# Norms and weights for layer 1's attention made inside layer 0's mixture of experts; batch 3's residual moved into the first global round

## The chip, the cores and the metric

One core of a Trainium2 chip runs the whole program. The metric is the device time of one execution in microseconds; lower is better. TensorE (PE) multiplies matrices and turns tiles, DVE (VectorE) and ACT (ScalarE) do elementwise work and read PSUM, POOL (GpSimd) does elementwise work in SBUF, SyncE (SP) issues the loads and stores. Each engine works through its own queue in order, and semaphores join them.

## The reference, cut to what matters

Two transformer layers over `x` of shape 4 x 1024 x 128, float32. Each block has the form x = x + layernorm(block(layernorm(x))):

```
x = x + LN(L0_attention(LN(x)))           # 16 heads of 64, causal
x = x + LN(L0_mixture(LN(x)))             # 8 routed experts (top 2) + 2 shared, SwiGLU, hidden 256
x = x + LN(L1_attention(LN(x)))           # below
x = x + LN(L1_soft_mixture(LN(x)))        # 8 x 64 slots

L1_attention(h):                          # 16 heads of 8, 4 key/value heads
  h = h + global_latent_attn(rmsnorm(h, norm1_w))   # keys and values through a latent of 32, causal
  h = h + local_gqa_attn(rmsnorm(h, norm2_w))       # causal window of 32
rmsnorm(h, w) = h * rsqrt(mean(h*h) + 1e-6) * w
```

So before the first product of layer 1's attention for batch 0 there stand: the mixture's output of batch 0 with its layer norm and residual, a layer norm of x, and the root mean square norm. The factor `w` of the latter is multiplied into the rows of the projection weights.

## The kernel before, in words

`x` stays in SBUF as 32 blocks of 128 rows (`g.x`); batch b is blocks 8b to 8b+7. The program is four stages in turn, each with its own tiles and semaphores and each a block of five engine programs. A barrier of all engines stands between two blocks: no engine starts the next stage before every engine has ended this one.

`mixture_layer0` runs 80 units: 4 batches x 10 experts x 2 halves of 512 rows. In unit u TensorE makes the up products of u (`raise_`, into 5 banks `m_up`) and the down product of u-1 (`lower`, `m_down`), ACT the SiLU, DVE `m_glu` (L1110) and the weighing of u-1 (L1122, into `acc` for a batch's first expert and into `part` for the rest), POOL adds `part` to `acc` (L850). DVE's list puts pieces of layer norms between the units, by the unit's number i within the batch: the residual of batch b-1 at i = 4 to 10, and the norm that makes the next batch's `x_norm` at i = 11 to 16. A norm has these pieces: four statistics pieces of two blocks each (L56), the variance (six small operations, L62 to L69), a root on POOL (L90), two pieces of four normalised blocks (L74). Batch 3's residual has no later units to sit in; it follows the last weighing (`residual(BATCH - 1)` at the end of DVE's program), its root at the end of POOL's.

`layer1_attention` works in 8 rounds of 32 steps: rounds 0 to 3 are global attention of batches 0 to 3, rounds 4 to 7 local attention. Round r makes scores and output of its own batch and prepares round r+1; the order is written out by hand, step by step, on each engine. "Round -1" prepares batch 0 alone: DVE makes the layer norm of x into `hidden`, squares, sums and scales it into `normed` (POOL: L90, L1378), multiplies the norm weights into `w_in` (L1712), TensorE turns `normed` (L1428), ACT copies it (L1615), then come the latent product (L1443), four quarters of projection (L1459, L1460), the rotation (L1738, L1384), the heads' norms, the slots' high and low parts and their turns, and the first scores (L1514). POOL zeroes `values` and the slots (L1366 to L1374) in this round, between its roots. SyncE loads 16 small tensors at the stage's start; ACT begins with `wait_ge(zeroed, 9)` and `wait_ge(loaded, 256)`. In rounds 0 to 2 the first norm of batch r+1 stands at steps 0 to 4, its squares, sum and scaling at steps 5 and 6. POOL cuts the diagonal block of each step (L1397) in rounds 0 to 3.

Of the kernel before, what the change touches and what calls it, by code (L numbers as in the profile page):

```python
# [15 lines left out]
P = 128  # L16
# [727 lines left out]

M_ORDER = [*range(E_ROUTED, EXPERTS), *range(E_ROUTED)]
# [8 lines left out]
RESIDUAL_ROOT_AT, NEXT_ROOT_AT = 6, 13  # L754
part_user = lambda u: u - 2 if place_of_unit(u) > 1 else u - 4

# [11 lines left out]
def mixture_layer0(nc, g):  # L768
    with ExitStack() as ctx:
# [16 lines left out]
        acc = sb("acc", [P, NBLK, D])  # L786
        gates = sb("gates", [P, NBLK, EXPERTS])
        norm = NormTiles(ctx, nc, "m_norm")
        lg = sb("lg", [P, NB, E_ROUTED])
# [14 lines left out]

        small_loaded, b3_loaded = sem("small_loaded"), sem("b3_loaded")
# [13 lines left out]
        cols_of = lambda b, c: slice(b * SEQ + c * HALF, b * SEQ + (c + 1) * HALF)  # L819
        as_blocks = lambda t: t[:].rearrange("p (t n) -> p t n", t=4)  # L820
# [3 lines left out]
        with nc.Block() as block:  # L824
            @block.sync
            def _(sp):
# [16 lines left out]
                sp.dma_start(b3[E_ROUTED:EXPERTS, :], g.inputs["L0_ffn_sb3"]).then_inc(b3_loaded, 16)  # L843

            @block.gpsimd
            def _(pool):
# [11 lines left out]
                for s in range(M_UNITS + 1):  # L858
                    u, i = s - 1, s % M_WINDOW
                    if s and place_of_unit(u):  # L860
                        pool.wait_ge(weighed, u + 1)
                        add(u, acc[:, blocks_of(batch_of_unit(u), half_of_unit(u)), :], part[u % 2][:])
                    for b, c in b3_added_at(s):
                        pool.wait_ge(b3_kept, b * 2 + c + 1)
                        add((b, c), acc[:, blocks_of(b, c), :], b3_part[c][:])
# [5 lines left out]
                assert roots + 1 == 2 * BATCH, roots  # L871
# [148 lines left out]
            def _(dve):  # L1020
# [15 lines left out]

                def residual(b):
# [75 lines left out]
                def weigh(u):  # L1113
# [8 lines left out]
                    dve.tensor_tensor(part[u % 2][:] if p else acc[:, blocks_of(b, c), :], as_blocks(down[u % 2]),  # L1122
# [48 lines left out]
HEADS, KV, HD = 16, 4, 8  # L1171
GQ = HEADS // KV
LAT = 32
# [5 lines left out]
RMS_EPS = 1e-6  # L1179
# [85 lines left out]
def layer1_attention(nc, g):  # L1265


    with ExitStack() as ctx:
# [6 lines left out]
        g.hidden = ctx.enter_context(nc.sbuf_tensor("hidden", [P, NBLK, D], F32))  # L1275
        norm1 = NormTiles(ctx, nc, "norm1")
        both = lambda name, shape, dt=F32: [sb(f"{name}{i}", shape, dt) for i in range(2)]
        w_in, w_o, norm_w = both("w_in", [P, 192]), both("w_o", [P, D]), both("norm_w", [P, 1])
        cos, sin = both("cos", [P, NB, HD // 2]), both("sin", [P, NB, HD // 2])
        w_up = sb("w_up", [LAT, 2 * KV * HD])  # L1280
        rows_of = sb("rows_of", [P, 2])
        normed = sb("normed", [P, NB, D])
# [22 lines left out]
        loaded, scaled, zeroed, chain = sem("loaded"), sem("scaled"), sem("zeroed"), sem("chain")  # L1305
# [37 lines left out]
        LOADS = 16  # L1343

        with nc.Block() as block:
            @block.sync
            def _(sp):
                for layer, (wq, wk, wo, nw, rope) in enumerate((
                        ("g_wq", "g_kv_down", "g_wo", "norm1_w", "c_rope_g"), ("l_wq", "l_wk", "l_wo", "norm2_w", "c_rope_l"))):
                    sp.dma_start(w_in[layer][:, 0:D], g.inputs["L1_attn_" + wq]).then_inc(loaded, 16)  # L1350
                    sp.dma_start(w_in[layer][:, D:D + 32], g.inputs["L1_attn_" + wk]).then_inc(loaded, 16)
                    sp.dma_start(norm_w[layer][:], g.inputs["L1_attn_" + nw].rearrange("(p a) -> p a", a=1)).then_inc(loaded, 16)
                    if layer == 0:
                        sp.dma_start(rows_of[:], g.inputs["c_rows_of"]).then_inc(loaded, 16)
                        sp.dma_start(w_in[1][:, D + 32:D + 64], g.inputs["L1_attn_l_wv"]).then_inc(loaded, 16)
                        sp.dma_start(w_up[:, 0:32], g.inputs["L1_attn_g_k_up"]).then_inc(loaded, 16)
                        sp.dma_start(w_up[:, 32:64], g.inputs["L1_attn_g_v_up"]).then_inc(loaded, 16)
                    sp.dma_start(cos[layer][:], g.inputs[rope][0].rearrange("(t p) n -> p t n", p=P)).then_inc(loaded, 16)
                    sp.dma_start(sin[layer][:], g.inputs[rope][1].rearrange("(t p) n -> p t n", p=P)).then_inc(loaded, 16)
                    sp.dma_start(w_o[layer][:], g.inputs["L1_attn_" + wo]).then_inc(loaded, 16)  # L1360

            @block.gpsimd
            def _(pool):
# [12 lines left out]
                def input_root(x):  # L1376
                    pool.wait_ge(ss_ready, x + 1)
# [1063 lines left out]
```

## Time and profile before

| | us |
|---|---|
| median of 3 runs | 2453.27 |
| lowest, highest | 2449.4, 2456.77 |
| the profiled execution | 2459.24 |
| its span, first to last instruction | 2457.5 |
| TensorE busy in the span | 2214.6 |
| DVE, ACT, POOL busy | 1459.5, 1229.4, 1054.8 |
| mean granted clock of TensorE | 0.959 |

The mixture's units end at 1548 us and the first scores of layer 1's attention are at 1611 us of the span. The granted clock is a share of 2.4 GHz: 1.00 is the full level, 0.50 the lower one of 1.2 GHz. In the timelines, equal instructions in a row are merged into one line with their count.

### The profile page before, as it was taken

How to read it: one execution, taken by the hardware profiler on the slowest of the kernel's cores; microseconds unless marked ns; L12 is line 12 of the kernel's file. 1: busy time of each engine (PE TensorE's matmuls, PEld its weight loads, DVE VectorE, ACT ScalarE, POOL GpSimd, SP SyncE). 2: the span in 40 equal slices, each digit the busy share in tenths (PEclk: the TensorE clock that was granted, in tenths of full speed). 3: DMA queues.
4: the chain of work that ended last, by engine and by line, in shares of the span. 5: the costliest groups of instructions: out<-in, count | busy, mean ns of one | idle time of the engine just before them, and what ended most of it. 6: DMA issues, size and time to landing. Idle time of an engine off the chain costs nothing. (4 is left out here: it accounts for less than half of the span.)

```text
span 2457.5 us, 40332 instructions
## 1 busy us (share of the span) xinstructions
PE 2214.6 (90%) x15428; PEld 1400.2 (57%) x15428; DVE 1459.5 (59%) x3240; ACT 1229.4 (50%) x1796; POOL 1054.8 (43%) x980
## 2 busy tenths in 40 slices
PE   4999999999999999985999999489999988876787
PEld 2555565556555565545888888334444455555667
DVE  3677758775777757753666666535545555545533
ACT  2555545554465535541333333167777866644543
POOL 0677757775677757771323223323322311100001
PEclk9999999999999999997999999679999999998999
DMA  2000000000000000002000000000000000003001
GB/s 74 1 1 1 1 1 1 1 1 1 1 1 1 1 1 1 1 1 65 1 1 1 1 1 1 7 1 1 1 1 1 1 1 2 2 3 74 1 1 35
DMA packets 36322, 18.19 MB, mean 7 GB/s; under 512 B 16666, under 2 KB 33956, under 8 KB 36132
## 3 DMA queue, kind: packets, MB, share of 16 engines
q1 hardware_dynamic: 36132, 15.61, 2.5%
q8 instruction: 125, 2.05, 0.4%
q14 instruction: 65, 0.53, 0.1%
HBM read 13.50 MB, written 2.10 MB: 6 GB/s over the span
## 5 line engine op out<-in xcount | busy, mean ns | idle before, releaser
L311 POOL TENSOR_TENSOR a_first<-a_first,a_ring 128x512 f32<-128x512 f32 (+3 forms) x352 | 559.3, 1589 | 142.2 <-ACT a_ring L556 106.9
L1645 ACT ACTIVATE g_probsT<-g_s_ps 128x1024 f32<-128x1024 f32 (+2 forms) x448 | 368.9, 869 | 143.2 <-PE g_s_ps L1514 89.0
L556 ACT ACTIVATE a_ring<-a_st 128x768 f32<-128x768 f32 (+1 forms) x256 | 234.8, 917 | 263.0 <-PE a_st L463 263.0
L478 PE MATMUL a_o_ps<-a_ring,a_v 128*64 128x512 f32 (+3 forms) x1280 | 249.2, 485 | 3.2 <-POOL a_ring L293 2.2
L645 DVE RECIPROCAL a_row_inv<-a_row_inv 128x512 f32<-128x512 f32 x64 | 213.9, 3343 | 16.8 <-ACT a_row_inv L544 16.8
L993 ACT ACTIVATE m_silu<-m_up,m_b 128x512 f32<-128x512 f32 x160 | 110.1, 688 | 220.8 <-PE m_up L927 220.7
L623 DVE TENSOR_REDUCE a_part_max<-a_mx 128x2 f32<-128x1024 f32 x128 | 156.6, 1223 | 103.2 <-PE a_mx L434 100.1
L1545 PE MATMUL g_o_ps<-g_probsT,g_values 128*32 128x512 f32 (+5 forms) x2688 | 213.1, 430 | 5.2 <-POOL g_probsT L1397 5.1
L850 POOL TENSOR_TENSOR m_acc<-m_acc,m_part 128x512 f32<-128x512 f32 x72 | 99.2, 1378 | 271.1 <-DVE m_part L1122 271.1
L1397 POOL TENSOR_SCALAR_AFFINE_SELECT g_probsT<-g_probsT 128x512 f32<-128x512 f32 x128 | 89.0, 698 | 255.2 <-ACT g_probsT L1645 255.0
L1514 PE MATMUL g_s_ps<-g_qT,g_kT 64*128 64x512 f32 (+3 forms) x896 | 173.9, 436 | 27.1 <-ACT g_probsT L1645 21.3
L1110 DVE SCALAR_TENSOR_TENSOR m_glu<-m_up,m_b,m_silu 128x512 f32<-128x512 f32 x160 | 119.4, 749 | 111.1 <-ACT m_silu L993 106.2
L630 DVE CUSTOM_DVE_ANT_0 a_masked<-a_mx,mask_wide,a_part_max 128x256 bf16<-128x256 f32 (+3 forms) x256 | 128.4, 548 | 92.8 <-PE a_mx L434 92.4
L630 DVE CUSTOM_DVE_ANT_0 a_masked<-a_mx,mask_wide 128x256 bf16<-128x256 f32 (+3 forms) x256 | 112.8, 488 | 82.9 <-PE a_mx L434 82.9
L1514 PEld LDWEIGHTS g_s_ps<-g_qT,g_kT 64*128 64x128 f32 x896 | 77.9, 189 | 143.4 <-ACT g_probsT L1645 94.9
L941 PEld LDWEIGHTS m_down<-m_w,m_glu 128*128 128x128 f32 x1280 | 155.0, 191 | 6.3
L941 PE MATMUL m_down<-m_w,m_glu 128*128 128x128 f32 x1280 | 155.5, 275 | 0.0
L463 PE MATMUL a_st<-a_q_hi,a_k_hi 64*128 64x512 f32 (+3 forms) x768 | 151.2, 387 | 3.9 <-ACT a_shift L534 3.1
L434 PE MATMUL a_mx<-a_k_hi,a_q_hi 64*128 64x512 f32 (+3 forms) x768 | 142.1, 391 | 12.0 <-DVE a_largest L630 11.3
L463 PEld LDWEIGHTS a_st<-a_q_hi,a_k_hi 64*128 64x128 f32 x768 | 73.5, 185 | 113.8 <-ACT a_ring L556 79.1
L927 PE MATMUL m_up<-m_xT_hi,m_w_hi 128*128 128x512 f32 x320 | 135.8, 425 | 1.4 <-DVE m_xT_lo L1062 1.4
L463 PE MATMUL a_st<-a_q_lo,a_k_hi 64*128 64x512 f32 (+3 forms) x768 | 135.9, 345 | 0.0
(287 smaller groups left out, 4373.7 us busy)
## 6 DMA issues: line engine op xcount, KB each, us to landing
m_w<-in_L_ffn_rw SPq DMA_DIRECT2D x2, 1024.0 KB, 8.4
s_w<-in_L_ffn_w SPq DMA_DIRECT2D x1, 2048.0 KB, 10.6
s_w<-in_L_ffn_w SPq DMA_DIRECT2D x4, 512.0 KB, 10.5
out_x<-x SPq DMA_DIRECT2D x8, 256.0 KB, 2.3
m_w<-in_L_ffn_rw SPq DMA_DIRECT2D x2, 512.0 KB, 5.2
x<-in_L_attn_x SPq DMA_DIRECT2D x1, 512.0 KB, 4.3
a_outT<-in_L_attn_w_q SPq DMA_DIRECT2D x1, 512.0 KB, 5.2
a_outT<-in_L_attn_w_k SPq DMA_DIRECT2D x1, 512.0 KB, 6.1
```

Source lines behind the costliest of these rows:

```text
L311: pool.tensor_tensor(total[:, h, q:q + w], total[:, h, q:q + w], probs_of(n, u)[:, h, off:off + w], ALU.add).then_inc(added, 1)
L434: last = pe.matmul(mx_ps[:, h, off:off + w], q_hi[m % 2][rows_of(h), i * P:(i + 1) * P], k_hi[m % 2][rows_of(h), key:key + w], start=True, ...
L463: last = pe.matmul(out[:, h, off:off + w], a[rows_of(h)], r[rows_of(h)], start=i == 0, stop=i == len(todo) - 1)
L478: last = pe.matmul(o_ps[rows_of(h), first_q:first_q + w], v_half[n // 4 % 2][:, j, head:head + A_HD], probs_of(n, u)[:, h, off:off + w], s ...
L556: act.activation(probs_of(n, u)[:, :, 0:w], st_ps[u % 2][:, :, 0:w], ACT.Exp).then_inc(exp_done, 1)
L623: last = dve.tensor_reduce(part_max[:, i, :], mx_ps[:], AX.X, ALU.max)
L630: last = dve.tensor_tensor_reduce(masked[1 - part][:, h, 0:w], mx_ps[:, h, off:off + w], g.mask_wide[:, HALF - w:HALF], 1.0, so_far, ALU.a ...
L645: dve.reciprocal(row_inv[c][:], row_inv[c][:]).then_inc(inv_ready, 1)
L941: last = pe.matmul(down[u % 2][:, t * P:(t + 1) * P], glu[u % 2][h][:, t * P:(t + 1) * P], w3[:, e, h, :], start=h == 0 and t == 0, stop=h ...
L1514: last = pe.matmul(out, kT[r % 2][s // 2][rows, kb * P:(kb + 1) * P], qT[r % 2][rows, j:j + at_once, a:e], start=True, stop=True, skip_gro ...
L1545: last = pe.matmul(o_ps[place * SLOT:(place + 1) * SLOT, a:e], values[r % 2][:, kb, head_at(s, place) // GQ, :], probsT[(r * STEPS + n) % ...
L1645: act.activation(out, src.rearrange("p k (j n) -> p k j n", j=at_once), ACT.Exp, scale=float(HD) ** -0.5).then_inc(exp_done, 1)
```

## The change

`hidden`, `normed` and the attention's weights are now allocated and loaded before the mixture ends: a class `AttentionWeights` holds the loads, and the mixture's SyncE program issues them last. `hidden`'s blocks of batch 3 serve as the accumulator of the mixture's batch 3 (`sums_of`), so its unfinished residual can be carried into the attention. In batch 3's units DVE now makes batch 0's layer norm (i = 11 to 16), squares (17), sum (18), scaling (19), and both weight scalings (11, 12); POOL makes the two roots. In the attention, round -1 starts at the turn of `normed`; POOL zeroes `values` and slots at its step 0; ACT waits for `zeroed` 4 before step 12 and 9 before step 18, DVE for 9 at step 18. Round 0 gets batch 3's residual at steps 8 to 14, with its root on POOL at step 10. The other first norms (batches 1, 2, 3) stay where they were.

```diff
 # mixture_layer0
-        acc = sb("acc", [P, NBLK, D])
+        acc = sb("acc", [P, NBLK - NB, D])
+        sums_of = lambda b, c: (acc if b + 1 < BATCH else g.hidden)[:, blocks_of(b, c), :]
 # SyncE, after b3
+                g.weights.load(sp, g, attention_loaded)
 # POOL
                     if s < M_UNITS and (i == RESIDUAL_ROOT_AT and s >= M_WINDOW
-                                        or i == NEXT_ROOT_AT and s < M_UNITS - M_WINDOW):
+                                        or i == NEXT_ROOT_AT):
...
-                inverse_root(pool, norm, g.minus_half[:, 0:NB], roots)
+                    if s == M_UNITS - M_WINDOW + RMS_ROOT_AT:
+                        pool.wait_ge(rms_ready, 1)
+                        pool.tensor_tensor(rms_root[:], rms_sum[:], g.minus_half[:, 0:NB], ALU.pow).then_inc(root_ready, 1)
 # DVE
+                def norms_of_attention():
...
+                    def square():
+                        chain.settle()
+                        own.did(dve.tensor_tensor(g.normed[:], first, first, ALU.mult))
+                    def sum_up():
+                        own.settle()
+                        own.did(dve.tensor_reduce(rms_sum[:], g.normed[:], AX.X, ALU.add))
+                        own.settle()
+                        dve.tensor_scalar(rms_sum[:], rms_sum[:], 1.0 / D, RMS_EPS, ALU.mult, ALU.add).then_inc(rms_ready, 1)
+                    def scale():
+                        dve.wait_ge(root_ready, 1)
+                        own.did(dve.tensor_tensor(g.normed[:], first, rms_root[:].unsqueeze(2).to_broadcast([P, NB, D]),
+                                                  ALU.mult))
+                    return layernorm_parts(dve, chain, x_of, out_of, norm, norms[0] - 1)[:-1] + [square, sum_up, scale]
...
-                        nexts = norm_of(b + 1) if b + 1 < BATCH else []
+                        nexts = norm_of(b + 1) if b + 1 < BATCH else norms_of_attention()
...
+                    if b + 1 == BATCH:
+                        for k in {17: (7,), 18: (8,), 19: (9,)}.get(i, ()):
+                            nexts[k]()
+                        if i in (11, 12):
+                            scale_weights(i - 11)
                 weigh(M_UNITS - 1)
-                for piece in residual(BATCH - 1):
-                    piece()
 # layer1_attention: SyncE's program removed. POOL
-                        if x < BATCH and n == 2:
-                            inverse_root(pool, norm1, g.minus_half[:, 0:NB], x)
-                            if r < 0:
-                                zero_values()
-                        if x < ROUNDS and n == (1 if is_local(r) else 5):
+                        if x in NORM_COUNT and n == 2:
+                            inverse_root(pool, norm1, g.minus_half[:, 0:NB], NORM_COUNT[x])
+                        if r == 0 and n == 10:
+                            inverse_root(pool, norm1, g.minus_half[:, 0:NB], 1)
+                        if r < 0 and n == 0:
+                            zero_values()
+                            zero_slots()
+                        if 0 < x < ROUNDS and n == (1 if is_local(r) else 5):
                             input_root(x)
-                            if r < 0:
-                                zero_slots()
 # TensorE: turn_input waits for normed_ready only if x > 0; the waits on `scaled` are gone. ACT
-                act.wait_ge(zeroed, 9)
-                act.wait_ge(loaded, LOADS * 16)
...
+                        if r < 0 and n == 12:
+                            act.wait_ge(zeroed, 4)
+                        if r < 0 and n == 18:
+                            act.wait_ge(zeroed, 9)
 # DVE
+                    left_over = residual(BATCH - 1, 1) if r == 0 else []
...
+                        if left_over:
+                            for i in {8: (0, 1), 9: (2, 3), 10: (4,), 12: (5,), 13: (6,), 14: (7,)}.get(n, ()):
+                                left_over[i]()
```

## Rows read from the trace of the kernel before

**Rows 1.** page, part 1: busy us, share of the span, instructions of each engine
```profile
PE 2214.6 (90%) x15428; PEld 1400.2 (57%) x15428; DVE 1459.5 (59%) x3240; ACT 1229.4 (50%) x1796; POOL 1054.8 (43%) x980
```

**Rows 2.** waits of TensorE: who waited, for whom: us in total, times, longest
```profile
PE g_x_ps L1428 <- DVE g_normed L1732: 23.0, 1, 23.0
...
PE g_x_ps L1428 <- DVE g_k_slots L1777: 16.0, 1, 16.0
```

**Rows 3.** timeline of TensorE at the seam: start, duration, what, count, [idle before]
```profile
1571.40 1.97 PE L1428 MATMUL g_x_ps<-ident,g_normed 128*128 128x128 f32 x8 [22.96 <-DVE g_normed L1732]
1575.32 3.42 PE L1443 MATMUL g_x_ps<-g_normedT,g_w_in 128*32 128x512 f32 x4 [1.96 <-ACT g_normedT L1615]
1578.67 0.49 PE L1459 MATMUL g_x_ps<-g_w_in,g_normedT 128*128 128x128 f32 x2
...
1581.79 0.77 PE L1459 MATMUL g_x_ps<-g_w_in,g_normedT 128*128 128x128 f32 x2
```

**Rows 4.** timeline of DVE at the seam
```profile
1548.48 0.69 DVE L1122 TENSOR_TENSOR m_part<-m_down,m_gates 128x512 f32<-128x512 f32 x1 [1.09 <-PE m_down L941]
...
1557.97 1.64 DVE L56 BATCH_NORM_STATS2 norm_stats<-x 128x6 f32<-128x128 f32 x8 [0.54 <-PEq L824]
...
1570.12 1.22 DVE L1732 TENSOR_TENSOR g_normed<-hidden,g_rs_h 128x1024 f32<-128x1024 f32 x1 [1.54 <-POOL g_rs_h L1378]
...
1587.91 0.83 DVE L1738 TENSOR_TENSOR g_part<-g_qk,g_cos 128x640 f32<-128x640 f32 x1 [13.25 <-ACT g_values L1624]
```

**Rows 5.** timeline of POOL at the seam
```profile
1547.46 1.27 POOL L850 TENSOR_TENSOR m_acc<-m_acc,m_part 128x512 f32<-128x512 f32 x1 [3.25 <-DVE m_part L1122]
1549.25 1.26 POOL L850 TENSOR_TENSOR m_acc<-m_acc,m_part 128x512 f32<-128x512 f32 x1 [0.52 <-DVE m_part L1122]
...
1560.55 1.64 POOL L90 TENSOR_TENSOR norm_rstd<-norm_var,minus_half 128x8 f32<-128x8 f32 x1 [6.55 <-DVE norm_var L69]
...
1570.92 3.63 POOL L1374 MEMSET g_q_slots<- 128x1024 f32 x4
```

**Rows 6.** timeline of ACT at the seam
```profile
1574.58 1.08 ACT L1615 ACTIVATE g_normedT<-g_x_ps 128x512 f32<-128x512 f32 x2 [28.99 <-POOL g_q_slots L1374]
```

**Rows 7.** seam by stretch: length, busy PE, PEld, DVE, ACT, POOL, granted clock, DMA
```profile
1551.00:1554.50 3.50, 0.00 (x0) 0.00 (x0) 1.64 (x11) 0.00 (x0) 1.65 (x1) 0.52 0.00 0
1578.50:1581.80 3.30, 3.30 (x18) 2.37 (x17) 0.00 (x0) 1.14 (x3) 0.00 (x0) 1.00 0.00 0
1581.80:1587.20 5.40, 5.39 (x17) 3.95 (x16) 0.00 (x0) 1.10 (x4) 0.00 (x0) 0.51 0.00 0
```

**Rows 8.** timeline of DVE, batches 2 and 3 of the mixture
```profile
1429.67 2.10 DVE L74 TENSOR_SCALAR m_x_norm<-x,m_norm_mean,m_norm_rstd 128x128 f32<-128x128 f32 x4
...
1505.45 1.21 DVE L1045 TENSOR_TENSOR x<-x,m_acc 128x1024 f32<-128x1024 f32 x1
```

**Rows 9.** timeline of POOL, batch 3 of the mixture
```profile
1505.61 2.21 POOL L850 TENSOR_TENSOR m_acc<-m_acc,m_part 128x512 f32<-128x512 f32 x1 [2.08 <-DVE m_part L1122]
```

**Rows 10.** busy time in batch 3 of the mixture
```profile
1457.00:1548.00 91.00, 91.00 (x566) 80.69 (x565) 54.88 (x115) 31.35 (x45) 26.55 (x20) 0.99 0.00 1
```

**Rows 11.** timeline of TensorE, batch 2 of the mixture
```profile
1427.08 1.95 PE L941 MATMUL m_down<-m_w,m_glu 128*128 128x128 f32 x16
...
1431.63 1.95 PE L941 MATMUL m_down<-m_w,m_glu 128*128 128x128 f32 x16
```

**Rows 12.** timeline of SyncE's queue, last load of the mixture
```profile
1154.46 0.24 SPq L843 DMA_DIRECT2D m_b<-in_L_ffn_sb  x1
```

**Rows 13.** timeline of TensorE, global rounds 1 to 3
```profile
1784.09 1.09 PE L1428 MATMUL g_x_ps<-ident,g_k_slots 128*128 128x128 f32 x8
...
1827.05 1.09 PE L1428 MATMUL g_x_ps<-ident,g_normed 128*128 128x128 f32 x8
...
1879.65 1.09 PE L1428 MATMUL g_x_ps<-ident,g_k_slots 128*128 128x128 f32 x8
...
1921.45 1.09 PE L1428 MATMUL g_x_ps<-ident,g_normed 128*128 128x128 f32 x8
```

More of the change, by code:

```diff
@@ L742 @@
 TOP = 8
+HEADS, KV, HD = 16, 4, 8
+GQ = HEADS // KV
+LAT = 32
+RMS_EPS = 1e-6
 M_ORDER = [*range(E_ROUTED, EXPERTS), *range(E_ROUTED)]
@@ L803, in mixture_layer0 @@
         aux = ctx.enter_context(nc.psum_tensor("m_aux", [P, HALF], F32))
+        attention_loaded, rms_ready, root_ready = sem("attention_loaded"), sem("rms_ready"), sem("root_ready")
         small_loaded, b3_loaded = sem("small_loaded"), sem("b3_loaded")
@@ L1035, in norm_of, with scale_weights @@
                     return layernorm_parts(dve, chain, x_of, lambda blk: x_norm[:, blk, :], norm, norms[0] - 1)
+                def scale_weights(layer):
+                    w, scale = g.weights.w_in[layer], g.weights.norm_w[layer]
+                    if layer == 0:
+                        dve.wait_ge(attention_loaded, g.weights.LOADS * 16)
+                    width = 192 if layer else 160
+                    own.did(dve.tensor_scalar(w[:, 0:width], w[:, 0:width], scale[:], None, ALU.mult))
+                def norms_of_attention():
+                    norms[0] += 1
+                    x_of, out_of = lambda blk: g.x[:, blk, :], lambda blk: g.hidden[:, blk, :]
+                    first = g.hidden[:, 0:NB, :]
+                    def square():
[11 more added lines that the diff above has]
+                    return layernorm_parts(dve, chain, x_of, out_of, norm, norms[0] - 1)[:-1] + [square, sum_up, scale]
                 def residual(b):
@@ L1121, in weigh @@
                         dve.wait_ge(added, M_ADDED[part_user(u)])
-                    dve.tensor_tensor(part[u % 2][:] if p else acc[:, blocks_of(b, c), :], as_blocks(down[u % 2]),
+                    dve.tensor_tensor(part[u % 2][:] if p else sums_of(b, c), as_blocks(down[u % 2]),
                                       gates[:, blocks_of(b, c), expert_of_unit(u)].unsqueeze(2).to_broadcast([P, 4, D]),
@@ L1178 @@
 LOCAL_W = P + WINDOW
-RMS_EPS = 1e-6
 STEPS = KV * NB
@@ L1303, in layer1_attention @@
         x_ps = [ctx.enter_context(nc.psum_tensor(f"g_x_ps{i}", [P, HALF], F32)) for i in range(2)]
-        loaded, scaled, zeroed, chain = sem("loaded"), sem("scaled"), sem("zeroed"), sem("chain")
+        zeroed, chain = sem("zeroed"), sem("chain")
         ss_ready, rs_ready, normed_ready = sem("ss_ready"), sem("rs_ready"), sem("normed_ready")
@@ L1341, in x_read @@
                 eng.wait_ge(x_read_dve, READS_DVE[k])
-        LOADS = 16
+        NORM_COUNT = {1: 0, 2: 2, 3: 3}
         with nc.Block() as block:
[L1346 to L1360, printed above, removed]
             @block.gpsimd
@@ L1447, in project @@
                     x_read(pe, "input", x, 0, quarter // 2)
-                    if is_local(x):
-                        pe.wait_ge(scaled, 2)
-                    else:
+                    if not is_local(x):
                         x_read(pe, "latent", x, 0, quarter // 2)
@@ L1791, in add @@
                         norm_chain.did(dve.tensor_tensor(batch, batch, hidden_of(x), ALU.add))
-                    return layernorm_parts(dve, norm_chain, y_of, y_of, norm1, x)[:-1] + [add]
+                    return layernorm_parts(dve, norm_chain, y_of, y_of, norm1, count)[:-1] + [add]
                 for r in range(-1, ROUNDS + 1):
@@ L1797, in _ @@
                     local = is_local(r)
-                    norm_parts = first_norm(x) if x < BATCH else []
-                    ends = residual(r - 1) if r > BATCH else []
+                    norm_parts = first_norm(x) if x in NORM_COUNT else []
+                    left_over = residual(BATCH - 1, 1) if r == 0 else []
+                    ends = residual(r - 1, r - 1) if r > BATCH else []
                     for n in range(STEPS):
@@ L1813, in _ @@
                                 sum_input(x)
-                                if r < 0:
-                                    dve.wait_ge(loaded, LOADS * 16)
-                                    scale_weights(0)
                             if n == (2 if local else 6):
                                 scale_input(x)
-                                if r < 0:
-                                    scale_weights(1)
-                                    dve.wait_ge(zeroed, 9)
+                        if x < ROUNDS:
+                            if r < 0 and n == 18:
+                                dve.wait_ge(zeroed, 9)
                             if n == (13 if local else 15):
```

66 lines of the change are left out of this document (42 added, 24 removed).

## The prediction

> **What bounds the kernel now.** I read the page first. TensorE is busy for 90% of the span [rows 1], so time is won only where TensorE stands still, or where its own work runs at the lower clock. The second view is the list of what TensorE waited for, longest first: the longest single wait of the whole kernel, 23.0 us, is its first turn of `g_normed` in layer 1's attention, released by DVE, and a second one of 16.0 us follows for `g_k_slots` [rows 2]. Only then did I read the timelines, engine by engine, over the seam from 1548 to 1611 us, to see what fills the 23 us.
>
> The last `m_down` ends at 1571.40 - 22.96 = 1548.44 us [rows 3]. From there everything is one serial chain of small operations. DVE weighs the last unit, POOL adds it (ends 1550.51), DVE and POOL make batch 3's layer norm and DVE adds the residual (ends 1557.44), then comes the barrier (0.54 us to DVE's next operation), then the layer norm of batch 0, its squares, sum, root, and the scaling that ends at 1571.34; TensorE starts at 1571.40 [rows 3 to 5]. Between POOL's last add and `g_normed` ready are 1571.34 - 1550.51 = 20.83 us, of which 0.54 is the barrier.
>
> TensorE then turns `g_normed` (1.97 us), but ACT starts its copy only at 1574.58, after 29.0 us of idleness that POOL's memset of `g_q_slots` ends [rows 5, 6]. So a second wait lies behind the first: the zeroing of nine tiles, which POOL queues behind its two roots. The latent product starts at 1575.32, 3.92 us after TensorE began, the projections at 1578.67, and DVE's rotation at 1587.91 [rows 3, 4].
>
> The clock is the third thing. TensorE is granted the lower level (1.2 GHz, mean 0.52) from about 1551.1 on, after some 2.7 us without a matmul, the full level (2.4 GHz, 1.00) from 1578.5 to 1581.8, and the lower one again to 1587.2 although it was busy for 5.39 of those 5.40 us [rows 7].
>
> **The change, part by part.** The sum is made on the profiled execution, 2459.24 us for its span of 2457.5, 5.97 above the median of the runs (2453.27); I carry the difference over to the median.
>
> (a) Removed from the seam: the residual of batch 3, batch 0's layer norm, square, sum, root, scaling, and both weight scalings. After the change the block ends when POOL's last add ends. In place of 1571.40, TensorE can start at 1550.51 + 0.54 = 1551.05. I take no extra time for TensorE itself to get through the barrier: no row shows it starting straight behind one, SyncE and DVE do in about 0.5 us. Bounds 0 to 1.5 us, the upper end by the nearest dearer seam step, POOL's own 1.64 us root [rows 5].
>
> (b) The scaling of `g_normed` now sits in the last unit between the last two weighings. DVE would start it at 1547.3 (it follows the weighing before last) and needs 1.22 us, so it ends at 1548.52, where the last weighing began at 1548.48 [rows 4]: 0.04 late. But POOL's add of unit 78 (1547.46, 1.27 us) falls on it [rows 5]. The same pair exists in batch 3: DVE's residual add of 1.21 us at 1505.45, and beside it a POOL add that took 2.21 us and ended 1.16 us after DVE's [rows 8, 9]. So POOL's add of unit 78 ends at 1548.52 + 1.16 = 1549.68, its last add at about 1551.0, and TensorE starts at 1551.0 + 0.54 = 1551.55. Cost 0.5 us; bounds 0 and 1.5 (if POOL goes first and DVE stands behind it, the weighing is 1.2 to 1.5 late).
>
> (c) The rest in batch 3's units: eight statistics (1.64), six small operations, two halves of the normalisation (2.10 each, with POOL running beside them), square (1.2), sum (1.2), two weight scalings (0.6 to 0.8 each, by a quarter of the 2.10 for each 128 columns), two more POOL roots (1.64 each), in nine units [rows 4, 5, 8]. TensorE is busy for all 91.0 us of batch 3 from 1457 on, DVE for 54.9 [rows 10]: over 20 units of 4.55 us DVE has 1.8 us to spare in each. In batch 2's units the same norm stands at the same places. There two `m_down` groups start at 1427.08 and 1431.63, 4.55 us apart, although DVE starts such a half of 2.10 us at 1429.67 [rows 8, 11]. Square and sum are shorter than 2.10. Price 0: what hides it is that slack, and five banks of `m_up`, which let a late `m_glu` pass. If the cover were gone, it would be what exceeds the gap, 0.7 us for each of five units, 3.5 in all. POOL waits for `rms_ready` in unit 18 with only the next add behind it, 4.55 us later. Bounds 0 to 3.5.
>
> (d) The sixteen loads go to SyncE's queue in the mixture, behind `b3`, whose last issue is at 1154.46 [rows 12]; at about 0.47 us each they are issued by 1162.3, nearly 350 us before DVE's wait for them. Everything the experts need is ahead of them in the queue. Price 0; bounds 0 and 1. Their removal at the seam brings nothing by itself: they were not waited for last.
>
> (e) ACT no longer waits for `zeroed`, 9 and the loads before its first copy. With TensorE starting at T, ACT starts after the first four turns, T + 1.15 (half of 1.97 and 0.17 to get there), copies in 0.6, and the latent product starts at T + 1.85 in place of T + 3.92: 2.07 us won [rows 3, 6]. What is late next is TensorE's own work. The zeroing itself begins at T: two `values` memsets and the small ones take 2.1 us, and ACT wants them at the first projection, T + 5.4; the slots' five take 4.6 and end at T + 6.7, ACT wants them past T + 25. Hidden.
>
> (f) The clock over the first products. TensorE stood still for 3.1 us instead of 23.0, yet the level fell at 1551.1, before 1551.55 [rows 7], so turns and latent product are priced cold: 1.85 + 3.42 = 5.25 us from T to the projections (7.27 before) [rows 3]. Four quarters of projection follow. Two at full level took 1581.79 - 1578.67 = 3.12 us, two at the lower 5.4 [rows 3, 7]; 0.7 to the rotation. All cold: 10.8. All warm: 6.2. As before, half and half: 8.5. I take 8.5, since the same instructions come in nearly the same order, with bounds 6.2 and 10.8. Rotation: T + 5.25 + 8.5 + 0.7 = T + 14.45 = 1566.0, in place of 1587.91: 21.9 us earlier.
>
> (The Trainium skill, TensorE: Matmul & The Clock Gate, HAM oscillation, says that a long enough idle gap sends the array back to the cold clock and each group after it starts cold. By that, too, the turns are cold; its Part 1, What's actually happening, would have the clock stay warm once sustained work has brought it up, and the projections would then all be warm. The trace speaks against this: the level fell again at 1581.8 amid dense work [rows 7].)
>
> (g) From the rotation to the first scores the same operations run in the same order: 0, but the clock's changes may fall otherwise. The difference of two quarters, 2.3 us either way, is the bound.
>
> (h) Round 0 gains batch 3's residual in steps 8 to 14: eight statistics, six small operations, eight normalisations, one add of 1.23 us (some 6 us of DVE) and one root of 1.64 on POOL. POOL's root stands ahead of the cut of step 11, and waits for a variance that DVE reaches only after reading the first latent bank: TensorE's second product of that pair may come late by a microsecond. The nearest rows are the rounds themselves. From the turn of `g_k_slots` to the next round's turn of `g_normed` it takes 1827.05 - 1784.09 = 42.96 us with a first norm inside (the same DVE and POOL work but the add), and 1921.45 - 1879.65 = 41.80 without one [rows 13]. So such a norm costs 1.16; I take 1.0. Bounds 0 and 4 (one more cut late by 1.6 and a spell of lower clock behind it).
>
> Sum: 21.9 - 1.0 = 20.9 us. 2459.24 - 20.9 = 2438.3 for the profiled execution, 2453.27 - 20.9 = 2432.4 for the median.
>
> **Rivals.**
> 1. *The clock stays up through the projections.* For: the stretch idle is 3.1 us, not 23. Against: the fall at 1581.8. Worth 8.5 - 6.2 = 2.3 more, with a share of the first products up to 4: 2453.27 - 23.2 = 2430.1, at the best 2426.
> 2. *The clock stays down throughout.* For: latent product and turns are now packed otherwise against the clock's changes, and in the whole of 1603 to 1611 it was down. 2.3 less: 2434.7.
> 3. *Moved work shows in round 0 and in batch 3.* A wait takes the place of the one removed: POOL stands at the root of step 10 while TensorE needs the next cut, and the units with a scaling slip. (c) 2 of 3.5 and (h) 3 to 4 give 4 to 5 less: about 2437.
> 4. *The work is on the path wherever it stands.* This ends on the other side. It has one place, DVE's queue ahead of `m_glu` and of the bank reads. If nothing there were slack, 11.5 us in batch 3, 6 to 8 in round 0 and POOL's roots of 5 would all lengthen TensorE's time, 24 in all, more than the 21.9 won: 2455 to 2456. It decides from the point where more than nine tenths of the moved work is uncovered. The 4.55 us distance of units with a norm in them speaks against it.
> 5. *The chain at the seam is not shortened as said*, because TensorE gets through the barrier much later than DVE, or the input is ready late: 5 us lost, 2437 to 2438.
>
> **How the numbers follow.** Forecast (with the clock half and half, round 0 at 0 to 2) 0.50; rival 1 0.17; rival 2 0.14; rival 3 0.12; rival 5 0.05; rival 4 0.02. The predicted time is 2432.4. Medians of three scatter by some 2 to 3 us (the three runs lie between 2449.4 and 2456.77), so the range takes rivals 1 and 2 with that scatter and most of 3: 2426 to 2439. About 0.3%, 7.4 us, is what a measurement can tell from no change. Only rival 4 and some mishap of two others reach that bound: faster 0.97, within 0.015, slower 0.015.
>
> **What the changed profile would show.** TensorE's wait for DVE's `g_normed` gone, and about 3 us of idleness in its place, ended by the barrier (a: wrong if over 5). POOL's add of unit 78 near 2.2 us (b). `m_down` groups of batch 3 still 4.55 us apart, the last matmul as early against the first of the mixture as before (c). ACT's first copy about 1.15 us after TensorE's first turn, not ended by a memset (e). The granted clock over the four quarters decides among 6.2, 8.5 and 10.8 (f). The `g_k_slots` wait still near 16 us. Round 0, from its first scores to round 1's turn of `g_normed`, longer by about 1 us (h). A total saving below 15 us or above 27 would make the prediction wrong.

## The result, and where the time went

The changed kernel runs in 2436.64 us (median of 5, 2429.34 to 2438.66), the kernel before in 2455.56 (median of 5, 2449.4 to 2456.77): ratio 0.9918, 95% interval 0.9896 to 0.9941, or 14 to 26 us. The medians are 18.9 us apart; forecast were 20.9. (A ratio in this document is that to the kernel before, run in the same series; the two numbers behind it are its 95% interval.) The two profiled executions, 2459.24 and 2429.34 us, are 29.9 apart. That is more than the change did, and the first thing to do was to cut both into stages that begin and end with the same instruction of TensorE:

| stage (us) | before | after | after, 2nd trace | after, 3rd |
|---|---|---|---|---|
| start to first turn of the mixture | 1147.4 | 1143.5 | 1145.9 | 1147.4 |
| to the end of the last `m_down` | 401.05 | 401.39 | 401.21 | 401.40 |
| **to the first scores** | **62.52** | **40.48** | **40.52** | **40.50** |
| to round 1's turn of `g_k_slots` (round 0) | 77.56 | 74.83 | 77.95 | 74.80 |
| to round 2's | 95.57 | 96.00 | 92.93 | 92.79 |
| to round 3's | 95.56 | 95.59 | 92.33 | 92.52 |
| to round 7's | 262.76 | 260.66 | 262.43 | 262.37 |
| to the end of the span | 315.09 | 315.15 | 315.10 | 314.90 |

The third row is the change: 22.0 us, the same in all three traces of the changed kernel within 0.04 (of the kernel before there is one trace). The rest are differences of up to 4 us that come and go between executions of the same kernel; within one series of runs the executions of either kernel spread over 6 to 16 us. Two later series gave 23.8 us (2432.97 against 2456.77) and 22.3 us (2430.67 against 2452.95) between the medians.

Of the 22.0 us, 20.0 are TensorE's shorter wait before its first turn, 1.85 the way from there to the projections, and the rest, 0.2, lies behind them.

TensorE's timeline at the seam after the change (columns as in [rows 3]); the last `m_down` ends at 1544.89:

```profile
1541.16 3.73 PE L980 MATMUL m_down<-m_w,m_glu 128*128 128x128 f32 x32
1547.84 1.94 PE L1476 MATMUL g_x_ps<-ident,normed 128*128 128x128 f32 x8 [2.95 <-PEq L860]
1549.71 3.62 PE L1491 MATMUL g_x_ps<-g_normedT,g_w_in 128*32 128x512 f32 x4
1553.26 0.80 PE L1505 MATMUL g_x_ps<-g_w_in,g_normedT 128*128 128x128 f32 x2
...
1557.48 0.79 PE L1505 MATMUL g_x_ps<-g_w_in,g_normedT 128*128 128x128 f32 x2
...
1577.57 1.94 PE L1476 MATMUL g_x_ps<-ident,g_k_slots 128*128 128x128 f32 x8 [16.00 <-DVE g_k_slots L1820]
```

TensorE now stands still for 2.95 us in place of 22.96 [rows 3], and what ends it is the barrier, not `g_normed`. The latent product follows the turns at once, where 1.96 us had been waited for ACT's copy. The stage's second wait, the last line, kept its 16.0 us [rows 2].

DVE, POOL and ACT over the same stretch, three timelines (rows that answer to [rows 4], [rows 5], [rows 6]):

```profile
1543.76 1.22 DVE L1100 TENSOR_TENSOR normed<-hidden,m_rms_root 128x1024 f32<-128x1024 f32 x1
1544.93 0.69 DVE L1190 TENSOR_TENSOR m_part<-m_down,m_gates 128x512 f32<-128x512 f32 x1
1562.26 0.82 DVE L1781 TENSOR_TENSOR g_part<-g_qk,g_cos 128x640 f32<-128x640 f32 x1 [16.63 <-ACT g_values L1670]
```
```profile
1543.92 3.58 POOL L887 TENSOR_TENSOR hidden<-hidden,m_part 128x512 f32<-128x512 f32 x2 [1.49 <-DVE m_part L1190]
1547.80 1.84 POOL L1413 MEMSET g_values<- 128x1024 f32 x2 [0.31 <-POOLq L860]
```
```profile
1548.96 0.60 ACT L1661 ACTIVATE g_normedT<-g_x_ps 128x512 f32<-128x512 f32 x1 [6.92 <-PE g_x_ps L1476]
```

DVE scales `normed` right before the last weighing; POOL's two adds, merged in one row, take 3.58 us where they took 1.27 and 1.26: the first, beside the scaling, takes 2.18, the second 1.26. ACT's copy starts 1.12 us after TensorE's first turn does, while POOL still zeroes.

The granted clock over turns and latent product, the middle of the projections, and their last part (columns as in [rows 7]):

```profile
1547.80:1553.20 5.40, 5.36 (x12) 2.10 (x12) 0.00 (x0) 1.78 (x3) 5.34 (x8) 0.50 0.00 0
1553.90:1557.40 3.50, 3.50 (x19) 2.66 (x18) 0.00 (x0) 1.16 (x5) 0.44 (x1) 0.98 0.00 0
1557.50:1561.50 4.00, 4.00 (x13) 2.97 (x12) 0.00 (x0) 0.55 (x2) 0.00 (x0) 0.50 0.00 0
```

The pattern is that of before: the lower level up to the projections, full in their middle, lower again although TensorE is busy for 4.00 of 4.00 us.

The moved work in batch 3's units, with TensorE's `m_down` groups around it (two timelines, as [rows 8] and [rows 11]):

```profile
1525.57 2.11 DVE L74 TENSOR_SCALAR hidden<-x,m_norm_mean,m_norm_rstd 128x128 f32<-128x128 f32 x4
...
1534.66 1.22 DVE L1090 TENSOR_TENSOR normed<-hidden 128x1024 f32<-128x1024 f32 x1
```
```profile
1522.98 1.95 PE L980 MATMUL m_down<-m_w,m_glu 128*128 128x128 f32 x16
...
1527.53 1.95 PE L980 MATMUL m_down<-m_w,m_glu 128*128 128x128 f32 x16
...
1532.07 1.95 PE L980 MATMUL m_down<-m_w,m_glu 128*128 128x128 f32 x16
...
1536.62 1.95 PE L980 MATMUL m_down<-m_w,m_glu 128*128 128x128 f32 x16
```

The groups stay 4.55 us apart, through a half of the normalisation of 2.11 us (between the first two) and the squares of 1.22 (between the last two).

### The profile page after: what moved, and what is told of

Its sections match the earlier page's. It is cut to its first block and busy times, and to the rows that moved or that the text cites. A ratio compares the mean times of both kernels' runs of the same rounds, so it can differ in the third digit from the quotient of the medians.

```text
span 2427.6 us, 40333 instructions
## 1 busy us (share of the span) xinstructions
PE 2205.2 (91%) x15428; PEld 1396.5 (58%) x15428; DVE 1457.3 (60%) x3240; ACT 1228.7 (51%) x1796; POOL 1056.3 (44%) x980
## 5 line engine op out<-in xcount | busy, mean ns | idle before, releaser
L887 POOL TENSOR_TENSOR m_acc<-m_acc,m_part 128x512 f32<-128x512 f32 x54 | 74.8, 1386 | 205.0 <-DVE m_part L1190 205.0
L463 PE MATMUL a_st<-a_q_hi,a_k_lo 64*128 64x512 f32 (+3 forms) x768 | 135.2, 344 | 0.0
```

The costliest lines, as they stand in the source:

```text
L463: last = pe.matmul(out[:, h, off:off + w], a[rows_of(h)], r[rows_of(h)], start=i == 0, stop=i == len(todo) - 1)
```

## Experiments

All are edits of the changed kernel; "stretch" is that from the last `m_down` to the first scores.

**1. The changed kernel again**, twice, to learn what repeats.

> The changed kernel once more, unaltered. Mine: the stretch from the last m_down to the first scores of the attention (62.5 us before the change, 40.5 after) is fixed by its chain and comes out at 40.5 within 0.3; the other stages, the 2.7 us less of round 0 among them, are the clock's changes falling otherwise and come out anew within 3 us. Rival: the 2.7 us less of round 0 (74.8 from first scores to the next turn of g_k_slots, against 77.6) belongs to the change and shows again within 0.3. Total 19 to 22 us below the kernel before by both.

> The changed kernel unaltered, as the partner of the two others in this call. Mine: TensorE idle for 2.95 us, the clock falls within them and the stretch is 40.5, as in its earlier traces; 4 to 5 us slower than the other two. Rival: the clock stays up here at times too, and then the stretch is 36.3.

Measured: stretch 40.52 and, in the later series, 40.50; round 0 77.95 and 74.80 (table above). The 22.0 us repeat. The first total lies 23.8 us below the kernel before, a little more than the 19 to 22 expected. The 2.7 us less in round 0 came in two of three traces, so they are not the change's. The second expectation held for the stretch, 40.50 with idleness of 2.95 us and the cold pattern, but not for the total: 2430.67 us lies 2.1 below that of experiment 6's version in the same series and 2.3 above the combination of experiment 7, not 4 to 5 above both.

**2. Batch 3's residual back at the seam.**

```diff
+                inverse_root(pool, norm, g.minus_half[:, 0:NB], roots)
...
                 weigh(M_UNITS - 1)
+                for piece in residual(BATCH - 1):
+                    piece()
...
-                        if r == 0 and n == 10:
-                            inverse_root(pool, norm1, g.minus_half[:, 0:NB], 1)
...
-                    left_over = residual(BATCH - 1, 1) if r == 0 else []
+                    left_over = []
```

> The changed kernel with batch 3's residual back behind the last weighing, at the seam. Mine: its layer norm, root and add stand in the chain with their full 6.9 us, so the stretch from the last m_down to the first scores is 47.4 (40.5 + 6.9), TensorE's idleness 9.8 in place of 2.95, and round 0 gives nothing back, since the residual lay hidden there: total 6.9 above the changed kernel. Rival from my prediction: round 0 gets 1 us shorter, total 5.9. Rival 2, that the chain was partly covered by the barrier and the start of TensorE: 4 to 5 in the stretch.

The added root stands at the end of POOL's program. Measured: 2440.93 us (ratio to before 0.994, 0.9916 to 0.9963), stretch 47.46, 6.94 more than the changed kernel's 40.52 in the same series (forecast 6.9); the medians are 8.0 apart. Round 0 took 77.87 us, against 77.95 with the residual in it. TensorE's first turn in its timeline waits 10.06 us, 7.1 more than 2.95:

```profile
1555.25 1.94 PE L1478 MATMUL g_x_ps<-ident,normed 128*128 128x128 f32 x8 [10.06 <-PEq L860]
```

The whole of this chain was on the path at the seam, and neither rival held.

**3. Batch 0's norms back in round -1.** The pieces `norms_of_attention` and POOL's two roots go from the mixture; `first_norm(0)`, `square_input(0)`, `sum_input(0)`, `scale_input(0)` and their roots come back.

> The changed kernel with batch 0's layer norm, squares, sum, root and scaling back in the attention's round -1 (the weight scalings stay in the mixture, the zeroing stands behind the two roots on POOL, ACT still waits late for it). Mine: 13.4 us of chain come back, less the 0.5 that the scaling costs in the last unit: 53.4 from the last m_down to the first scores; the mixture's batch 3 gets no shorter than by 0.4. Rival: the moved work cost TensorE time among the units too (up to 3.5), then batch 3 is shorter by that and the total rises by only 10.

Measured: 2440.30 us (0.9943, 0.9922 to 0.9964), 7.3 above the changed kernel of the same series; stretch 50.75, not 53.4. TensorE's idleness is what was forecast, 15.85 us, 12.90 more than 2.95. What gave 2.7 us back is the clock: 0.9 between first turn and projections, 1.8 in the projections. TensorE's first turn, and the granted clock over latent product and projections of this kernel:

```profile
1564.50 1.97 PE L1472 MATMUL g_x_ps<-ident,normed 128*128 128x128 f32 x8 [15.85 <-DVE normed L1770]
```
```profile
1566.40:1569.00 2.60, 2.60 (x5) 0.47 (x4) 0.00 (x0) 1.18 (x2) 1.25 (x2) 0.68 0.00 0
1569.00:1575.50 6.50, 6.50 (x33) 4.92 (x32) 0.00 (x0) 2.24 (x7) 0.00 (x0) 0.95 0.00 0
```

The full level came early in the latent product and stayed through the projections (mean 0.95), all four in 6.5 us. Without batch 0's norm in them, batch 3's units and the rest of the mixture took 401.52 us, with it 401.39, 401.21 and 401.40: the moved work cost TensorE nothing there.

**4. ACT waits for all nine memsets first.**

```diff
                 HIGHS = {18: 0, 19: 1, 20: 2, 21: 3, 22: 4}
+                act.wait_ge(zeroed, 9)
```

> The changed kernel, but ACT waits for all nine memsets before its first copy, as it did before the change. Mine: the memsets end 6.6 us after TensorE's start, ACT's first copy starts then in place of at 1.1, so the stretch from the last m_down to the first scores is 5.5 longer: 46.0. That is more than the 2.07 us that this wait cost in the kernel before, as the norms no longer hide it. Rival: it costs about 2 us, as it did, since the cold clock stretches what TensorE does in between anyway.

Measured: 2438.49 us (0.9925, 0.9902 to 0.9949), stretch 48.35, 7.8 more, not 5.5. ACT's copy starts 6.53 us after the first turn:

```profile
1547.88 1.94 PE L1476 MATMUL g_x_ps<-ident,normed 128*128 128x128 f32 x8 [2.95 <-PEq L860]
1555.15 3.59 PE L1491 MATMUL g_x_ps<-g_normedT,g_w_in 128*32 128x512 f32 x4 [5.34 <-ACT g_normedT L1661]
```
```profile
1554.41 1.08 ACT L1661 ACTIVATE g_normedT<-g_x_ps 128x512 f32<-128x512 f32 x2 [12.33 <-POOL g_q_slots L1421]
```
```profile
1555.10:1569.50 14.40, 14.31 (x36) 8.52 (x36) 0.00 (x0) 3.22 (x10) 0.00 (x0) 0.50 0.00 0
```

The wait cost 5.4, as forecast (POOL's memsets end 6.5 us after TensorE's start), and 2.4 more went to the clock, which stayed at the lower level for latent product and projections alike. So the rival's 2 us did not hold: the early copy was worth 5 us or more once the norms no longer hid the zeroing, though its row before showed only 2 us.

**5. The residual left out** (statistics to add; batch 3's output is then not the reference's).

```diff
-                    left_over = residual(BATCH - 1, 1) if r == 0 else []
+                    left_over = []
...
-                        if r == 0 and n == 10:
-                            inverse_root(pool, norm1, g.minus_half[:, 0:NB], 1)
```

> The changed kernel without batch 3's mixture residual (its statistics, variance, root, normalisation and add in round 0 are left out, so batch 3 is computed wrongly). Mine: round 0 (from first scores to the next turn of g_k_slots) stays at one of its two lengths, 74.8 or 77.6 to 78.0, as the clock falls, and TensorE's waits in it are the same; the total stays within 1 us of the changed kernel. Rival, the term of my prediction: round 0 is 1 us shorter than at the same clock, 73.8.

Measured: 2433.0 us (0.9921, 0.9889 to 0.9952). The changed kernel was not run in this series, so that the total stays within 1 us of it is not shown. Round 0 took 76.17 us, neither of the two lengths expected, so length alone doesn't settle it. Length beside the granted clock does. Round 0 as one stretch, in the order with residual (the changed kernel, then `zero_first`) and without (this one, then `residual_back`):

```profile
1585.37:1660.20 74.83, 66.62 (x493) 28.18 (x493) 43.08 (x109) 56.10 (x64) 27.11 (x31) 0.95 0.00 1
```
```profile
1593.27:1670.81 77.54, 70.18 (x492) 28.95 (x493) 43.07 (x109) 56.07 (x64) 27.19 (x31) 0.90 0.00 1
```
```profile
1591.11:1667.28 76.17, 67.97 (x493) 28.60 (x493) 37.12 (x86) 56.15 (x64) 25.60 (x30) 0.93 0.00 1
```
```profile
1592.65:1670.52 77.87, 69.88 (x493) 28.82 (x493) 37.37 (x86) 56.12 (x64) 25.63 (x30) 0.91 0.00 1
```

With it DVE is busy for 43.1 us, without for 37.1 to 37.4; the round's length goes with the clock instead. TensorE's idleness, the length less its busy time, is 8.21 us in the first line (with) and 8.20 in the third (without). At equal clock: the kernel before, without, 77.56 at 0.90, and `zero_first`, with, 77.54 at 0.90; `residual_back`, without, 77.87 at 0.91, and the second trace of the changed kernel, with, 77.95 at 0.91. TensorE's two longest waits in round 0 (us in total, times, longest) are the same with it (first) and without:

```profile
PE g_s_ps L1560 <- ACT g_probsT L1691: 6.3, 9, 1.6
PE g_o_ps L1591 <- POOL g_probsT L1444: 1.5, 1, 1.5
```
```profile
PE g_s_ps L1558 <- ACT g_probsT L1689: 6.3, 9, 1.6
PE g_o_ps L1589 <- POOL g_probsT L1444: 1.5, 1, 1.5
```

**6. Everything one unit earlier in batch 3**, so that no scaling stands in the last unit; run in two series.

```diff
-RESIDUAL_ROOT_AT, NEXT_ROOT_AT, RMS_ROOT_AT = 6, 13, 18
+RESIDUAL_ROOT_AT, NEXT_ROOT_AT, RMS_ROOT_AT = 6, 13, 17
...
-                        for k in {11: (0, 1), 12: (2, 3), 13: (4,), 15: (5,), 16: (6,)}.get(i, ()):
+                        late = {15: (5,), 16: (6,)} if b + 1 < BATCH else {14: (5,), 15: (6,)}
+                        for k in ({11: (0, 1), 12: (2, 3), 13: (4,)} | late).get(i, ()):
...
-                        for k in {17: (7,), 18: (8,), 19: (9,)}.get(i, ()):
+                        for k in {16: (7,), 17: (8,), 18: (9,)}.get(i, ()):
```

> The changed kernel with the two halves of batch 0's normalisation, the squares, the sum and the scaling each one unit earlier in batch 3 (14 to 18 in place of 15 to 19). Mine: no DVE work stands between the last two weighings, POOL's add of unit 78 is back at 1.3 us in place of 2.2, and TensorE's idleness at the seam goes from 2.95 to 2.4; stretch from the last m_down to first scores 40.0. Rival: POOL's last add is late for another reason (the second of the two adds itself), and it stays 2.95.

> The kernel of unit_earlier once more (batch 0's scaling out of the last unit; TensorE idle for 2.42 us at the seam). There the granted clock did not fall, and the stretch from the last m_down to first scores was 35.7 in place of 40.5. Mine: this belongs to the shorter idleness and comes again: 35.7, with the clock at the full level through turns, latent product and projections; total 4 to 5 us below the changed kernel of the same call. Rival: it was chance how the idleness of 2.4 us fell against the clock's changes; in some runs the clock falls as with 2.95 us, and the stretch is 40.0, the total 0.5 to 2.5 below.

Measured: first series 2428.46 us (0.9913, 0.9882 to 0.9944), stretch 35.73; second series 2432.74 (0.9915, 0.9889 to 0.9941), stretch 37.24. POOL's two adds and TensorE in the first trace, then TensorE in the second, the first trace's granted clock up to the projections' end (columns as in [rows 7]), and last the second trace's granted clock just before and behind the start of its first turn:

```profile
1544.56 1.27 POOL L887 TENSOR_TENSOR hidden<-hidden,m_part 128x512 f32<-128x512 f32 x1 [2.33 <-DVE m_part L1190]
1546.34 1.26 POOL L887 TENSOR_TENSOR hidden<-hidden,m_part 128x512 f32<-128x512 f32 x1 [0.51 <-DVE m_part L1190]
```
```profile
1547.95 1.06 PE L1477 MATMUL g_x_ps<-ident,normed 128*128 128x128 f32 x8 [2.42 <-PEq L860]
1549.36 1.88 PE L1492 MATMUL g_x_ps<-g_normedT,g_w_in 128*32 128x512 f32 x4 [0.34 <-ACT g_normedT L1662]
```
```profile
1551.41 1.94 PE L1477 MATMUL g_x_ps<-ident,normed 128*128 128x128 f32 x8 [2.42 <-PEq L860]
1553.28 2.65 PE L1492 MATMUL g_x_ps<-g_normedT,g_w_in 128*32 128x512 f32 x4
```
```profile
1547.90:1551.20 3.30, 2.90 (x13) 1.25 (x13) 0.00 (x0) 1.67 (x3) 3.23 (x6) 1.00 0.00 0
1551.30:1557.50 6.20, 6.16 (x32) 4.58 (x32) 0.00 (x0) 2.21 (x7) 3.15 (x4) 1.00 0.00 0
```
```profile
1551.30:1551.41 0.11, 0.00 (x0) 0.03 (x1) 0.00 (x0) 0.00 (x0) 0.04 (x1) 1.00 0.00 0
1551.41:1551.50 0.09, 0.09 (x1) 0.09 (x2) 0.00 (x0) 0.00 (x0) 0.09 (x1) 0.51 0.00 0
```

The adds are back at 1.27 and 1.26, as expected, and the idleness at 2.42 us in both. The stretch missed the expected 40.0: the 4.8 us less of the first trace are 0.53 of idleness and 4.2 of clock, which did not fall at all before the projections ended. In the second trace it stayed at the full level through the 2.42 us and fell just as the turns began, and they took 1.94 in place of 1.06. So my expectation for the repeat fell. Its rival was right that the clock may fall here too, but not in the numbers: the stretch is 37.24, not 40.0, as the full level was back for the projections, and the total lies 2.1 above the changed kernel of its series, not below it.

In the traces with 2.95 us of idleness or more, read in windows of 0.1 us, the clock fell 2.1 to 2.7 us after the end of the last `m_down` (changed kernel: 2.34, 2.15 and 2.36; kernel before: 2.69). TensorE resumed at 2.42 here, in the midst of these, and at 2.95 in the changed kernel, behind them all. What decides it at 2.42 us, these two traces don't show.

**7. Extra matmuls that keep TensorE busy.** Eleven behind the last `m_down`; then eight, together with edit 6.

```diff
                 lower(M_UNITS - 1)
+                for _ in range(11):
+                    pe.matmul(up[0][:], w_hi[:, 0, 0, 0:P], xT_hi[:, 0:HALF], start=True, stop=True)
```

> The changed kernel with eleven more matmuls of 128x512 (2.5 us in all, into a bank nobody reads) on TensorE behind the last m_down, while POOL's adds end. Mine: what the 3 us of idleness cost is the clock. With it bridged the turns and the latent product run at the full level: 3.3 us from the first turn to the projections in place of 5.4, and the projections at 6.2 to 8.4; stretch from the last m_down to first scores 37 to 38.5. Rival: the clock falls on the turns themselves, a weak load, so the granted clock is at the lower level by the latent product again, and less than 1 us is won.

> unit_earlier with eight extra matmuls of 128x512 (1.9 us) behind the last m_down as well. Mine: TensorE is idle for some 0.5 us, the clock stays up in every run, stretch 35.7 as in unit_earlier; total equal to unit_earlier within 0.5 if the clock stays up there by itself, up to 4 us faster in the median if there it does so only at times. Rival: the extra matmuls overrun POOL's end and cost their excess, up to 0.5.

Measured: 2428.24 us (0.9897, 0.9864 to 0.993), stretch 36.34, below the 37 to 38.5 expected; and 2428.40 (0.9894, 0.9868 to 0.9921), stretch 37.49, above the 35.7 expected. TensorE with eleven:

```profile
1550.01 2.78 PE L1005 MATMUL m_up<-m_xT_hi,m_w_hi 128*128 128x512 f32 x11
1553.27 1.06 PE L1478 MATMUL g_x_ps<-ident,normed 128*128 128x128 f32 x8 [0.48 <-PEq L860]
1554.67 1.88 PE L1493 MATMUL g_x_ps<-g_normedT,g_w_in 128*32 128x512 f32 x4 [0.34 <-ACT g_normedT L1663]
1556.48 0.49 PE L1507 MATMUL g_x_ps<-g_w_in,g_normedT 128*128 128x128 f32 x2
```

Idle for 0.48 us, it turns in 1.06 and has the latent product in 1.88 instead of 3.62; from first turn to projections 3.2 us instead of 5.4, and all four quarters of projection run at the full level. In the combination (idleness 0.60 us) the clock also stayed up until after the projections had begun, then fell inside them, so it did not stay up in every run as expected. The changed kernel of the same series as the combination gave 2430.67 (0.9908, 0.988 to 0.9935); in the other series it was not run. The stretch is 4.2 and 3.0 us shorter in the two traces, but the intervals of the totals overlap, so no version is shown to beat the changed kernel.

**8. The same in the 16 us before the turn of `g_k_slots`.**

```diff
+                    if n == 20:
+                        pe.wait_ge(qk_var, 1)
+                        for _ in range(6):
+                            pe.matmul(o_ps[:, 0:HALF], normedT[:, 0:P], normedT[:, 0:HALF], start=True, stop=True)
                     fill_banks(-1, n)
```

> The changed kernel with six more float32 matmuls of 128x512 on TensorE in the 16 us in which it waits for g_k_slots (behind DVE's variance of the heads, into the bank of the outputs, which is overwritten later). Mine: they take 7 to 8 us of those in which TensorE waits, the clock is at the full level when the turns of g_k_slots begin, these take 1.1 in place of 1.94, the next eight are still held by ACT, and the first scores come 1 to 1.5 us earlier (39 to 39.5 in the stretch); round 0 is 2 us shorter at its start. Rival: the turns and the 2 us of idleness between them let the clock fall before the scores, as in the kernel before after 1587, and nothing is won beyond 1 us. If the matmuls overrun the wait, it gets longer by what they overrun.

Measured: 2431.36 us (0.9917, 0.9892 to 0.9943), stretch 40.47, nothing won. TensorE's timeline (the six matmuls are twelve instructions in the trace), and the granted clock over the turns of `g_k_slots` and the last twelve of `g_q_slots`:

```profile
1572.83 8.03 PE L1639 MATMUL g_o_ps<-g_normedT 128*128 128x512 f32 x12 [7.65 <-DVE g_ssq L1794]
1581.20 1.07 PE L1476 MATMUL g_x_ps<-ident,g_k_slots 128*128 128x128 f32 x8 [0.33 <-DVE g_k_slots L1824]
1584.24 0.66 PE L1476 MATMUL g_x_ps<-ident,g_q_slots 128*128 128x128 f32 x4 [1.98 <-ACT g_kT L1661]
...
1588.99 0.73 PE L1560 MATMUL g_s_ps<-g_qT,g_kT 64*128 64x512 f32 x4 [0.69 <-ACT g_qT L1663]
```
```profile
1581.20:1582.30 1.10, 1.07 (x8) 0.83 (x8) 0.85 (x2) 1.10 (x5) 0.00 (x0) 1.00 0.00 0
1585.40:1588.30 2.90, 2.90 (x12) 2.27 (x12) 0.00 (x0) 1.62 (x3) 0.00 (x0) 0.50 0.02 6
```

The turns of `g_k_slots` take 1.07 in place of 1.94, and TensorE then waits 1.98 us for ACT's copies in place of 1.10: the next turns start 3.04 us after these, as against 3.05. So ACT's copies set the pace up to there. Behind them the clock was at the lower level again, the last twelve turns took 2.91 us, and ACT waited for TensorE (0.72, 0.26 and 0.35 us before its last three copies). The rival held: nothing was won.

## Why the prediction held, step by step

(a) Held. Residual 6.94 us by experiment 2 (forecast 6.9), norms 12.90 of idleness by experiment 3 (13.4 less 0.5). TensorE passes the barrier 0.34 us after POOL's last add (1547.84 less 1547.50); I had taken 0.54 from a row in which DVE came last.

(b) Held: the add of unit 78 took 2.18 us (forecast near 2.2), POOL's adds end 2.61 us after the last `m_down` (2.56), TensorE's idleness is 2.95 (3.11), and experiment 6 takes back 0.53 of it (0.5). That this half microsecond could decide whether the clock falls before the first turn was not in the forecast.

(c), (d) Held: from its first turn to the last `m_down` the mixture takes 401.2 to 401.4 us in the three traces of the changed kernel (401.05 before), 401.23 with the residual back and 401.52 with the norms back, and nothing waits for the loads. Two other traces, the second of experiment 6 and the first of experiment 7, have 404.4; the same code of experiment 6 took 401.02 in its other trace, so that is not the moved work. It is the clock: over the 20 us that begin 100 us after the first turn, experiment 6's two traces have a mean of 0.83 and 1.00, which is 3.4 us, and the lower level came there while TensorE was busy throughout. The price of 0.7 us a unit, had the slack not covered the moved work, follows from no row: the halves of 2.10 us exceed 1.8 us to spare by 0.3. That (d) cost nothing was seen in the traces only; no experiment moves the loads back.

(e), (f) Held: first turn to projections 5.42 us (forecast 5.25; its terms, 1.85 + 3.42, add up to 5.27), first turn to rotation 14.42 (14.45), the projections half cold and half warm as before. That it would be half and half was the weakest step. The changed kernel and experiments 3, 4 and 6 show all three cases that I had listed, for the same instructions: four quarters warm in 6.2 to 6.5, half and half in 8.3, all cold in 10.8. Rival 1 and rival 2 were real, only not in this kernel's traces.

(g) Held: 23.11 us from rotation to scores, 23.05 before.

(h) Mis-sized: forecast 1.0, measured 0.0 within 0.1 (experiment 5). I had read 42.96 against 41.80 us in [rows 13] as the price of a norm anywhere in a round. In the kernel before, 1.1 of those 1.2 us are one wait of TensorE for POOL's cut behind the root of the squares (L1378), 1.42 us in the round with the norm and 0.29 in the one without; round 0 has it too, 1.48 us, with the residual or without. The three waits, two from before and one from after:

```profile
1823.52 0.43 PE L1545 MATMUL g_o_ps<-g_probsT,g_values 128*32 128x128 f32 x8 [1.42 <-POOL g_probsT L1397]
...
1917.53 0.43 PE L1545 MATMUL g_o_ps<-g_probsT,g_values 128*32 128x128 f32 x8 [0.29 <-POOL g_probsT L1397]
```
```profile
1609.97 0.43 PE L1591 MATMUL g_o_ps<-g_probsT,g_values 128*32 128x128 f32 x8 [1.48 <-POOL g_probsT L1444]
```

The residual comes behind that root and adds no such wait. The cut of step 11, which I feared for, came out in time: POOL's root ran at 1620.89 and TensorE did not wait for it.

The sum by the trace is 22.0 us; the forecast of 20.9 is 1.1 short, 1.0 of it by (h). How near the medians come to it is in part luck: the three series gave 18.9, 23.8 and 22.3, a scatter wider than the miss. The profiled execution, forecast at 2438.3, took 2429.34, and of the 9.0 us less 7.9 lie outside the seam. Rivals 3, 4 and 5 fall with (c), (h) and (a).

What remains open: which load on TensorE lets the granted clock fall. It was at the lower level amid the projections, where TensorE was busy for 4.00 of 4.00 us, and after 2.42 us of idleness it fell in one trace of two.

## What to carry to other kernels

Read a seam as a chain from the last product of one stage to the first of the next, and look for the second wait behind the first: the late copy showed as 2 us in the trace of before and was worth 5.4 once the norms in front of it were gone. Work of 16 us (11.9 on DVE, 4.4 on POOL, by their busy time in batch 3 before and after) cost TensorE nothing among units in which DVE had 1.8 us to spare each. Compare traces by stages with the same end instructions before believing their totals: here 8 of 29.9 us belonged to neither kernel.

## What the runs showed of the hardware

The same eight matmuls of a turn took 1.06 or 1.94 us, the same four quarters of projection 6.2 to 10.8, by the granted clock alone. After idleness of 2.95 us it was at the lower level in all three traces of this kernel and in those of experiments 4, 5 and 8; after 2.42 in one of two; after 0.48 and 0.60, the rest filled with extra matmuls, in neither of two. POOL's add beside a DVE product of two SBUF tiles took 2.18 us in place of 1.27. It goes the other way too: in the kernel before, DVE's eight normalisations of batch 0 took 3.43 us, with POOL's memset of `values` (1.84 us) started beside them, and those of batch 3's residual, with POOL idle, 2.14.
